# Softmax weights and shares of the last layer of a graph network, held in a PSUM bank in place of SBUF

## The reference, cut to what matters

```
h = x @ W
a_src = h @ att_src
a_dst = h @ att_dst
e = jax.nn.leaky_relu(a_src[src] + a_dst[dst], NEG_SLOPE)
m = jax.ops.segment_max(e, dst, num_segments=N)
e = jnp.exp(e - m[dst])
denom = jax.ops.segment_sum(e, dst, num_segments=N)
alpha = e / (denom[dst] + 1e-16)
out = jax.ops.segment_sum(h[src] * alpha[:, None], dst, num_segments=N)
x = _layernorm(x + jnp.tanh(out + bias))
```

## Time and profile before

| what | value |
|---|---|
| median of 3 runs | 4266.56 us (4257.02 to 4273.81) |
| profiled execution, span from first to last instruction | 4261.0 us |
| own time of the profiled execution | not listed beside its span; the span lies inside the range of the three runs and 5.6 us under their median |
| busy share over the span: DVE, POOL, PE, ACT | 66%, 64%, 45%, 44% |
| last layer, from its first gather to the end of the span | 3107.4 to 4261.0 us |
| granted TensorE clock over the span | 0.659 |

### The profile page before, as it was taken

The page is one execution under the profiler, slowest core; times in us unless marked ns, Lnnn a source line. Parts: engine busy times, 40 slices in busy tenths (PEclk is TensorE's granted clock), DMA queues, the critical chain, the costliest instruction groups (busy, mean ns, idle before and its releaser), DMA issues. The chain is left out here.

```text
span 4261.0 us, 39832 instructions
## 1 busy us (share of the span) xinstructions
PE 1919.8 (45%) x8382; PEld 1417.5 (33%) x8382; DVE 2819.2 (66%) x10490; ACT 1859.7 (44%) x3815; POOL 2740.4 (64%) x2760
## 2 busy tenths in 40 slices
PE   5578634777766666644444357777710000000000
PEld 2244103666654554522222157777700000000000
DVE  8899854777765655568878767777655545454545
ACT  8699102656642222224444446565632323232323
POOL 7366656666646666656666466666457666676766
PEclk9899556877778777766666556666655555555555
DMA  1111764555545555545566444444322222222221
GB/s 51 49 35 36 213 203 111 145 135 138 143 122 178 181 173 177 179 139 181 180 187 185 145 135 164 152 157 158 125 77 72 65 72 68 68 69 67 72 65 51
DMA packets 380540, 524.65 MB, mean 123 GB/s; under 512 B 221914, under 2 KB 255983, under 8 KB 380042
## 3 DMA queue, kind: packets, MB, share of 16 engines
q1 hardware_dynamic: 286154, 366.89, 26.1%
q0 software_dynamic: 94144, 155.21, 15.4%
HBM read 230.36 MB, written 291.54 MB: 122 GB/s over the span
## 5 line engine op out<-in xcount | busy, mean ns | idle before, releaser
L1632 POOL DMA_INDIRECT l_G<-t,src x391 | 415.0, 1061 | 228.3 <-issue 104.6
L1949 POOL DMA_INDIRECT out<-O,nidx x392 | 393.4, 1004 | 229.3 <-issue 110.9
L1311 POOL DMA_INDIRECT l1a_G<-t,src x391 | 376.5, 963 | 232.1 <-issue 111.7
L2167 PE MATMUL l_psR<-l_diag,l_ones 128*128 128x128 f32 x2 | 0.8, 501 | 1131.2 <-DVE l_diag L2031 1131.2
L1932 POOL DMA_INDIRECT l_G<-t,src x391 | 403.2, 1031 | 166.7 <-issue 118.2
L1311 POOL DMA_INDIRECT l1b_G<-t,src x391 | 380.2, 972 | 197.7 <-issue 110.4
L642 POOL DMA_INDIRECT O<-x_pad,nidx x344 | 326.7, 950 | 188.9 <-DMA O<-x_pad,nidx 97.0
L975 POOL DMA_INDIRECT l_G<-xs,src x327 | 310.3, 949 | 169.0 <-issue 88.4
L2167 PEld LDWEIGHTS l_psR<-l_diag,l_ones 128*128 128x128 f32 x2 | 0.5, 310 | 1131.3 <-DVE l_diag L2031 1131.3
L207 ACT ACTIVATE O<-O,l_shift,l_rstd 128x96 f32<-128x96 f32 x784 | 291.2, 453 | 27.2 <-DVE l_shift L201 27.2
L1989 DVE TENSOR_TENSOR l_e<-l_G,l_to_score 128x8 f32<-128x8 f32 (+3 forms) x51 | 8.5, 166 | 444.2 <-DMA l_G<-t,src 444.2
(11 more groups left out here) (350 smaller groups left out, 6554.5 us busy)
## 6 DMA issues: line engine op xcount, KB each, us to landing
h<-l_G SPq DMA_DIRECT2D x96, 392.0 KB, 2.4
t<-l1b_t_out SPq DMA_DIRECT2D x48, 768.0 KB
h<-l_G SPq DMA_DIRECT2D x48, 768.0 KB, 3.8
xs<-en_y SPq DMA_DIRECT2D x48, 392.0 KB, 3.7
t<-l_t_out SPq DMA_DIRECT2D x48, 392.0 KB
l_H<-t SPq DMA_DIRECT2D x48, 392.0 KB, 3.2
en_y<-x_pad SPq DMA_DIRECT2D x48, 384.0 KB, 4.9
t<-l_tr_out SPq DMA_DIRECT2D x48, 384.0 KB
```

Of the source, the lines that this page charges most:

```text
L1311: pool.indirect_dma_start(tile(c)[:, q, :], None, table, bass.IndirectOffsetOnAxis(k.src[:, at:at + 1], 0))\
L1632: pool.indirect_dma_start(tile(c)[:, q, :], None, table, bass.IndirectOffsetOnAxis(k.src[:, at:at + 1], 0))\
L1949: pool.indirect_dma_start(out, bass.IndirectOffsetOnAxis(k.nidx[:, at:at + 1], 0), k.O[:, at, :], None, bounds_check=NP - 1, oob_is_err=Fa ...
```

## The change

The two SBUF tiles are dropped. In their place a fourth one-bank PSUM tensor, psW, is allocated, and `ex` and `share` become views of it: 64 and 32 numbers of a partition, side by side. With it the layer uses all eight banks. No instruction is added, removed or moved, and no wait is changed.

```diff
         dd = sb("dd", [128, 2, 4, Q])
-        ex = sb("ex", [128, 2, 4, Q])
         mx = sb("mx", [128, 2, Q])
-        share = sb("share", [128, 2, 2, Q])
         total = sb("total", [128, Q])
...
-        psR, psX, psF = ps("psR"), ps("psX"), ps("psF")
+        psR, psX, psF, psW = ps("psR"), ps("psX"), ps("psF"), ps("psW")
+        ex = psW[:, 0:8 * Q].rearrange("p (u i q) -> p u i q", u=2, i=4)
+        share = psW[:, 8 * Q:12 * Q].rearrange("p (u i q) -> p u i q", u=2, i=2)
         psY = ctx.enter_context(nc.psum_tensor("l3_psY", [128, 1024], F32))
```

## The result

The kernel after takes 4220.7 us, the median of 4 runs (4211.18 to 4224.27), against 4266.31 us for the kernel before on the same chip. The ratio is 0.9885, with a 95% interval of 0.9864 to 0.9907. The forecast was 4226.6 us, its range 4213 to 4246. The profiled execution has a span of 4222.5 us, 38.5 less than before. Its first 3106.3 us, up to the last layer's first gather, are 1.1 us shorter than before; from there to the end it takes 1116.2 us against 1153.6. So 37.4 us of the 38.5 are in the last layer, where the change is.

A forecast was written before the change was run, and what follows sets the result against it. POOL's serial chain was taken to bound the last layer: 46.5 us of excess less 5.5 that stays gives 41, less 1 for phases, PSUM cost 0, so 4266.56 - 40 = 4226.6 us; range 4213 to 4246 us.

The forecast's parts named there:

- The bound: Last layer: POOL's serial scatters, gathers and landing wait set the pace; a microsecond off a POOL instruction shortens the layer equally.
- The stall and its cause: L2016, L2077, L2081 stall POOL by reading two SBUF tensors; one input in PSUM removes it entirely, 41 us.
- The sum: Last layer: 46.5 us of POOL excess over medians, 5.5 stays, 41 goes, 1 off for phases: gain 40 us.
- 1 for phases: Last layer: 1 us taken off the 41 us of stall because the phases change.
- What stays: POOL's excess in the last layer that remains: first scatters and gathers, second scatters, start and end rows; together 5.5 us.
- I subtract nothing for it: L2026 keeps two SBUF inputs, but a 0.97 us scatter inside it shows no stop, so 0 us counted.
- The period from first scatter to first scatter: Last layer, chunk to chunk: to become 0.9 us shorter on the mean.
- The PSUM accesses: Operations on psW: added cost hidden in VectorE's idle time except at the kernel's end; bounds 0 and +7 us, taken as 0.
- The time: Whole kernel: span 4221 us, median 4226.6 us, 0.94% less; full gain given chance 0.78.
- the first one: Last layer: some stalls stay or return in L2026, L1993 and small operations; gain 20 us, 4247 us; chance 0.11.
- The half-speed broadcast out of PSUM: L2016 and L2081: broadcast PSUM read at half speed with POOL still held; +50 us, 4316 us; chance 0.03.
- the partial gain: Last layer: only L2081's or half of all collisions freed; gain 20 us, 4247 us; chance 0.11.

The follow-up runs named there:

- share_only: Kernel after with ex put back in an SBUF tile, so only share stays in PSUM; ratio 0.9924 to the kernel before.
- ex_only: Kernel after with share put back in an SBUF tile, so only ex stays in PSUM; 4249.9 us, ratio 0.9960 to the kernel before.
- nb_sbuf: Kernel after with the neighbours' product in an SBUF tile instead of PSUM, so L2083 reads two SBUF tensors, neither broadcast; ratio 0.9920 to the kernel before.
- d_two_sbuf: Kernel after plus four spare 128x768 VectorE operations per full chunk, both inputs in SBUF, a drain after each; ratio 0.9994 to the kernel before.
- d_psum: Kernel after plus four spare 128x768 VectorE operations per full chunk, first input in PSUM, second in SBUF; 4234.8 us, ratio 0.9925 to the kernel before.
- d_short: Kernel after plus 24 spare 128x96 VectorE operations per full chunk, two SBUF inputs, a drain after every eighth; 4254.8 us, ratio 0.9974 to the kernel before.
- l2_split: Kernel after with the third layer's L1675 split into eight 128x96 operations with the same inputs; 4226.3 us, ratio 0.9903 to the kernel before.
- d_phase: d_two_sbuf with five spare operations of 128x576 in place of its four of 128x768; ratio 0.9987 to the kernel before.
- d_copy: Kernel after plus six spare 128x768 float32 copies per full chunk, SBUF to SBUF, a drain after each; ratio 0.9933 to the kernel before.

## Why the prediction was right

- **The bound.** That POOL's chain sets the pace and has no slack held: rows shorter by 38.4 us, layer by 37.4. The pair without the landing wait shows it again with 48.1 and 48.1.
- **The stall and its cause.** The step from "POOL's row ends 0.84 us after VectorE's" and from L1334 to "one input in PSUM frees it" was right for all three operations, and share_only, ex_only, nb_sbuf and the pair d_two_sbuf and d_psum leave neither the broadcast, nor the addresses, nor VectorE's load as a cause. The Trainium skill's page "SBUF — State Buffer", section "Who interferes with whom", says that two SBUF inputs contend with a GpSimd instruction that reads SBUF. The runs agree: POOL's indirect transfers take their node numbers from SBUF, and d_two_sbuf has gathers of up to 1.72 us where d_psum has 0.94.
- **The sum.** 41 us of stall less 1 for phases, against 38.4 measured. What stays is 8.1 us (373.2 - 369.1 and 385.0 - 381.0) in place of 5.5. Two terms were short. One is "I subtract nothing for it", said of L2026: with POOL earlier, 20 scatters take 1.03 to 1.06 us, as at 3506.56 above, each starting 0.11 to 0.14 us into an operation of L2026; before, three did. That is about 1.2 us more. The other is the second gather of a chunk, 0.968 us on the mean with nothing in its way, which the list of what stays leaves out: 45 x 0.024 = 1.1 us. The period from first scatter to first scatter fell by 0.77 us (23.38 to 22.61 on the mean), not 0.9.
- **The PSUM accesses.** Taken at 0 between 0 and 7 us; the end is 0.14 us longer. Of VectorE's operations on psW none is slower by more than the 0.008 us of L2068 (0.175 to 0.183 us), and ScalarE's write of the exponentials (L2122) takes 0.20 us in place of 0.23. The Trainium skill's page "VectorE: DVE Perf Modes", section "The TRN2 errata", gives 120 cycles of fixed cost with a PSUM source against 58 from SBUF; these rows show no such difference.
- **The time.** The gain of the medians, 45.6 us, is above the 40 forecast; the interval of the ratio reaches from 40 to 58 us, and the profiles say 38.5. The profiles are the test of the mechanism; how near the median came to 4226.6 us is partly the spread of the runs.
- **The rivals.** None came at its price. What the first one described, POOL's scatters coming under L2026, did happen, and cost about 1 us in place of 20. The half-speed broadcast out of PSUM is refuted by 954 and 962 ns, the partial gain by the missing long rows. My picture of the hold was too simple, though: it is not just "until the operation ends", and two expectations built on that (d_short, l2_split) missed. The sizes for d_two_sbuf and nb_sbuf missed because of the phases, that for d_phase because each gather was held for less.

## What to carry to other kernels

Where GpSimd's indirect transfers are the bound, look at which VectorE operations its long rows start in, and what those read. If both inputs are in SBUF, moving one into a spare PSUM bank frees GpSimd, and here it cost nothing that the rows show. It pays also when VectorE has idle time to spare. Moving only the result doesn't help (L2077 writes PSUM and held gathers all the same). Cutting the operation into back-to-back pieces gained nothing in the third layer; pieces with a pause after each hardly held anything. And when the bounding engine waits in each round for something it doesn't need yet, it pays nearly all of it: here that wait was worth two and a half times the stall.

## What was not expected of the hardware

- A POOL instruction that starts within 0.04 us after the start of a long VectorE operation with two SBUF inputs is free (0.94 us), and one that starts 0.05 us or more after it is held, up to 1.77 us. The closest pair is in the third layer of the kernel before, under L1675, and it shows the other side too: where the gather is free, VectorE's row is 0.10 us longer.

```profile
2648.70 1.03 DVE L1675 TENSOR_TENSOR l_inv<-l_inv,l_G 128x768 f32<-128x768 f32 x1
2648.74 0.95 POOL L1632 DMA_INDIRECT l_G<-t,src  x1 [0.30 <-issue]
...
2673.59 0.93 DVE L1675 TENSOR_TENSOR l_inv<-l_inv,l_G 128x768 f32<-128x768 f32 x1
2673.64 1.69 POOL L1632 DMA_INDIRECT l_G<-t,src  x1 [0.30 <-issue]
```

- Which of the two happens is a matter of phase, and the phase repeats: in the kernel before, chunks mostly alternate between the same two patterns.
- Short VectorE operations without a pause between them can hold like one long one (2.02 us for a gather under eight of 0.25 us), but let through other POOL instructions after 0.1 us or less. With a pause after each they hold by 0.1 us at most.
- A float32 copy with a single SBUF input, 0.584 us for 768 elements, holds too (d_copy).
- Ahead of L2009, which has two SBUF inputs, VectorE sits idle for 0.22 us, 23 times in the kernel before; 22 of these times a POOL instruction starts 0.02 to 0.05 us into L2009, and that row mostly takes 0.22 to 0.24 us in place of 0.16. The longer row fits a VectorE that gives way to POOL; what the idle time comes from, no run here shows.
